# Recommender tower on one core: a quarter's pieces in another order on every engine, norms between bias and variance, the last layers five quarters sooner

## What is computed

```python
e = stack([tbl_f[ids[:, f]] for f in range(26)], axis=1)     # (2048, 26, 64)
x = layer_norm(dense @ Wd.T, gd, bd)                         # (2048, 128)
y = layer_norm(einsum('bnd,ed->bne', e, Ws), gs, bs)         # per sample and feature
y = einsum('bne,pn->bep', y, Wsi)                            # 26 features mixed to 32
y = swapaxes(layer_norm(y, gsi, bsi), 1, 2)
T = concatenate([x[:, None, :], y], axis=1)                  # (2048, 33, 128)
Z = einsum('bnd,bmd->bnm', T, T)                             # pairwise products
z = layer_norm(Z[:, TRIL_I, TRIL_J] @ Wl.T, gl, bl)[:, :384]
h = concatenate([z, dense], axis=1)
h = maximum(h @ W_top1 + b_top1, 0.0)
h = maximum(h @ W_top2 + b_top2, 0.0)
out = h @ W_top3                                             # (2048, 1)
```

## Time and profile before

| | |
|---|---|
| median of 3 runs | 1021.42 us (1021.18 to 1025.5) |
| the profiled execution | 1019.76 us, its span 1018.0 us |
| busy in the span | PE 657.4 us (65%), PEld 474.9 (47%), DVE 530.4 (52%), ACT 279.4 (27%), POOL 423.3 (42%) |
| mean granted TensorE clock | 0.79 |
| DMA | 20.19 MB, mean 20 GB/s |

### The profile page before, as it was taken

The page is one execution under the profiler, slowest core; times in us unless marked ns, Lnnn a source line. Parts: engine busy times, 40 slices in busy tenths (PEclk is TensorE's granted clock), DMA queues, the critical chain, the costliest instruction groups (busy, mean ns, idle before and its releaser), DMA issues.

```text
span 1018.0 us, 17199 instructions
## 1 busy us (share of the span) xinstructions
PE 657.4 (65%) x6955; PEld 474.9 (47%) x6955; DVE 530.4 (52%) x769; ACT 279.4 (27%) x666; POOL 423.3 (42%) x422
## 2 busy tenths in 40 slices
PE   2034535364767757677775767768577776788887
PEld 2033324243444534446453545545355454566566
DVE  2248455454654535465453546545355654588740
ACT  1201122122232322233231323322132332345332
POOL 6757534545443344543345453433545343300000
PEclk9999676686776768777676778767687776799899
DMA  6111001010000011100001110000110010000000
GB/s 163 32 19 27 19 15 20 19 21 17 15 20 14 18 19 21 19 13 18 14 19 19 22 18 13 19 14 19 19 22 16 13 21 14 14 3 2 1 2 1
DMA packets 22606, 20.19 MB, mean 20 GB/s; under 512 B 12016, under 2 KB 14720, under 8 KB 22528
## 3 DMA queue, kind: packets, MB, share of 16 engines
q0 software_dynamic: 13312, 13.66, 7.4%
q1 hardware_dynamic: 8400, 4.33, 1.7%
q10 hardware_dynamic: 816, 1.11, 0.3%
HBM read 19.07 MB, written 0.01 MB: 19 GB/s over the span
## 4 chain that ended last, share of the span: by engine, by line
another core or an unknown queue 29%; PE 27%; issue 22%; DVE 14%; ACT 7%; ACTq 0%; DVEq 0%; POOL 0%; POOLq 0%
PE b_y L340 6%; PE b_l L416 5%; PE b_a L319 4%; DVE yb L781 3%; PE b_l L394 3%; DVE byn L776 2%; PE b_z L352 2%; ACT sq L508 2%; PE b_l L423 2%; DVE nrm L767 2%; PE b_mix L328 2%; DVE prod L747 1%; PE b_a L310 1%; ACT embt L492 1%
## 5 line engine op out<-in xcount | busy, mean ns | idle before, releaser
L253 POOL DMA_INDIRECT emb<-in_tbl,idx x416 | 422.6, 1016 | 453.7 <-DVE nrm L767 333.5
L319 PE MATMUL b_a<-gram_w,embt 128*128 128x128 f32 x416 | 85.3, 361 | 135.6 <-ACT embt L492 65.1
L793 DVE RECIPROCAL rstd_y<-std_y 128x32 f32<-128x32 f32 x64 | 21.2, 331 | 270.0 <-ACT std_y L513 269.9
L352 PE MATMUL b_z<-V 128*32 128x34 f32 x4096 | 91.3, 206 | 96.7 <-issue 89.6
L319 PEld LDWEIGHTS b_a<-gram_w,embt 128*128 128x128 f32 x416 | 71.9, 257 | 149.6 <-ACT embt L492 76.4
L508 ACT ACTIVATE sq<-yb 128x1024 f32<-128x1024 f32 x64 | 67.7, 1057 | 265.8 <-DVE yb L781 219.7
L328 PE MATMUL b_mix<-mix,byn 128*128 128x128 f32 x512 | 103.3, 334 | 39.8 <-issue 38.9
L352 PEld LDWEIGHTS b_z<-V 128*32 128x32 f32 x4096 | 67.6, 114 | 121.7 <-issue 107.8
L788 DVE TENSOR_REDUCE var_y<-sq 128x32 f32<-128x1024 f32 x64 | 78.1, 1220 | 71.9 <-ACT sq L508 47.2
L328 PEld LDWEIGHTS b_mix<-mix,byn 128*128 128x128 f32 x512 | 88.5, 239 | 48.3 <-issue 47.4
L340 PE MATMUL b_y<-mixed,projw 64*128 64x512 f32 x256 | 99.2, 862 | 15.2 <-ACT mixed L503 14.9
(11 more groups left out here) (131 smaller groups left out, 759.2 us busy)
## 6 DMA issues: line engine op xcount, KB each, us to landing
emb<-in_tbl,idx POOLq DMA_INDIRECT x416
dense<-in_r_dense_t SPq DMA_DIRECT2D x16, 128.0 KB
V<-in_L_rec_Wl ACTq DMA_DIRECT2D x1, 1056.0 KB
w<-in_W_top SPq DMA_DIRECT2D x2, 512.0 KB
w<-in_W_top SPq DMA_DIRECT2D x1, 768.0 KB
out_y<-y_sb SPq DMA_DIRECT2D x16, 0.5 KB
idx<-in_ids SPq DMA_DIRECT2D x1, 195.0 KB
wd<-in_L_rec_Wd SPq DMA_DIRECT2D x1, 128.0 KB
```

Source lines behind the costliest of these rows:

```text
L253: pool.indirect_dma_start(out=emb[t % 2][:, f, :], out_offset=None, in_=tables[f], in_offset=bass.IndirectOffsetOnAxis(ap=idx[:, t, f:f + ...
L319: last = nc.tensor.matmul(b_a[:, n * P:(n + 1) * P], embt[:, n, :], gram_w[:, :], start=True, stop=True)
L352: last = nc.tensor.matmul(b_z[32 * q:32 * q + 32, GRAM * j:GRAM * (j + 1)], v[:, 0:NP], v, start=True, stop=True)
```

## The change

No instruction is added or removed; the same ones run in another order and under other waits.

- PE: `mix_features` ahead of `transposes`; `gram` of the previous part is no longer last but stands ahead of `project`; `interact_back` directly behind `project`, ahead of `norms`; `layer3` ahead of `interact`.
- DVE: `add_bias`, then `norms` and `bound_n`, then `variance`, then `normalize` of the half just measured, `by_sample`'s second part, and `scale` of the same part, in the same quarter. `shuffle` is cut in two calls, the second at the start of the next quarter; `by_sample` too.
- ACT: `copy_mixed` ahead of `copy_embt`; `copy_zs`, `scale_x`, `scale_o` and `copy_z` ahead of `square_y`; `deviation_y` of the same part behind it.
- The constants: PAIRS 12 to 11, INTERACT 13 to 12, INTERACT_NORM 14 to 13, with `interact_back` in that quarter, LAYER1 18 to 13, LAYER2 20 to 15, LAYER3 21 to 16, STORE 22 to 17: 78 quarters in place of 83. `dt` has 4 buffers in place of 5, `xt` 2 in place of 3, and the waits that protect shared banks follow.

The core of the diff:

```diff
-PAIRS = 12
-INTERACT = 13
-INTERACT_NORM = 14
-INTERACT_BACK = 15
-LAYER1 = 18
-LAYER2 = 20
-LAYER3 = 21
-STORE = 22
+PAIRS = 11
+INTERACT = 12
+INTERACT_NORM = 13
+LAYER1 = 13
+LAYER2 = 15
+LAYER3 = 16
+STORE = 17
...
             def dense_back(t):
                 pe.wait_ge(xn_done, t + 1)
+                after(pe, zt_copied, 2 * (t - 1))
...
             def pair_rows(t):
 
                 pe.wait_ge(zb_ready, 3 * (t + 1))
-                after(pe, zz_copied, t)
+                after(pe, h1_relued, 4 * (t - 1) + 2)
...
-                if ab:
-                    transposes(*ab)
                 if bc:
                     mix_features(*bc)
                 if ab:
-                    norms(*ab)
+                    transposes(*ab)
+                if cc:
+                    gram(*cc)
                 if bc:
                     project(*bc)
+                if (t := tile(h, INTERACT_NORM)) is not None:
+                    interact_back(t)
+                if ab:
+                    norms(*ab)
...
                 if (t := tile(h, DENSE)) is not None:
                     dense_project(t)
-                if cc:
-                    gram(*cc)
...
+            def by_sample(t, k):
...
+                if (t := tile(h, INTERACT_NORM)) is not None:
+                    scale_o(t)
                 if (t := tile(h, DENSE)) is not None:
                     copy_dt(t)
+                if (t := tile(h, INTERACT_NORM)) is not None:
+                    copy_z(t)
                 if bc:
                     square_y(*bc)
                 if ab and ab[1] % 2:
                     deviation_n(ab[0], ab[1] // 2)
+                if bc:
+                    deviation_y(*bc)
...
                 if (t := tile(h, DENSE_NORM)) is not None:
                     moments_x(t)
-                    normalize(t, 0)
                 if (t := tile(h, SHUFFLE)) is not None:
-                    normalize(t, 1)
-                    shuffle(t)
-                if cc:
-                    scale(*cc)
+                    shuffle(t, 1)
+                if (t := tile(h, PAIRS)) is not None:
+                    by_sample(t, 0)
                 if (t := tile(h, INTERACT_NORM)) is not None:
                     recip_o(t)
                 if (t := tile(h, DENSE_NORM)) is not None:
                     recip_x(t)
+                if bc:
+                    add_bias(*bc)
+
                 if ab:
                     norms(*ab)
                     if ab[1] % 2:
                         bound_n(ab[0], ab[1] // 2)
                 if bc:
-                    add_bias(*bc)
                     variance(*bc)
+
+                if ab and ab[1] % 2:
+                    normalize(ab[0], ab[1] // 2)
+                if (t := tile(h, PAIRS)) is not None:
+                    by_sample(t, 1)
+                if bc:
+                    scale(*bc)
+                if (t := tile(h, SHUFFLE - 1)) is not None:
+                    shuffle(t, 0)
```

More of the change, by code:

```diff
@@ L359, in dense_transposes @@
                 after(pe, x_copied, 2 * t)
-                after(pe, zt_copied, 2 * (t - 2))
                 for f in range(2):
@@ L369, in dense_project @@
                 for f in range(2):
-                    last = nc.tensor.matmul(b_x[:, 2 * P:3 * P], dt[t % 5][:, f, :], wdt[:, f, :], start=(f == 0), stop=(f == 1))
+                    last = nc.tensor.matmul(b_x[:, 2 * P:3 * P], dt[t % 4][:, f, :], wdt[:, f, :], start=(f == 0), stop=(f == 1))
                 last.then_inc(x_projected, 1)
@@ L406, in layer1 @@
                 pe.wait_ge(zz_copied, t + 1)
-                if k == 0:
-                    pe.wait_ge(zt_copied, 2 * min(t + 2, T))
-                    after(pe, y_copied, t)
-                else:
-                    pe.wait_ge(z_ready, min(t + 2, T))
                 for m in (2 * k, 2 * k + 1):
@@ L453, in _ @@
                     pair_rows(t)
+                if (t := tile(h, LAYER3)) is not None:
+                    layer3(t)
                 if (t := tile(h, INTERACT)) is not None:
                     interact(t)
-                if (t := tile(h, LAYER3)) is not None:
-                    layer3(t)
                 if (t := tile(h, LAYER1)) is not None:
                     layer1(t, 0)
-                if (t := tile(h, INTERACT_BACK)) is not None:
-                    interact_back(t)
                 if (t := tile(h, LAYER1 + 1)) is not None:
@@ L498, in deviation_n, with deviation_y, deviation_x, deviation_o @@
                 nc.scalar.activation(std_n[:, f[0]:f[-1] + 1], var_m[:, f[0]:f[-1] + 1], ACT.Sqrt, bias=eps[:, 0:1]).then_inc(stdn_done, 1)
+            def deviation_y(t, c):
+                act.wait_ge(vary_done, 4 * t + c + 1)
+                after(act, rstdy_done, 4 * t + c - 1)
+                nc.scalar.activation(std_y[c % 2][:, :], var_y[c % 2][:, :], ACT.Sqrt, bias=eps[:, 0:1]).then_inc(stdy_done, 1)
+            def deviation_x(t):
+                act.wait_ge(x_step, 2 * (t + 1))
+                after(act, x_rstd, t)
+                nc.scalar.activation(sd_x[:, :], mv_x[:, 1:2], ACT.Sqrt, bias=eps[:, 0:1]).then_inc(x_std, 1)
+            def deviation_o(t):
+                act.wait_ge(o_step, 2 * (t + 1))
+                after(act, o_rstd, t)
+                nc.scalar.activation(sd_o[:, :], mv_o[:, 1:2], ACT.Sqrt, bias=eps[:, 0:1]).then_inc(o_std, 1)
             def copy_mixed(t, c):
@@ L508, in square_y @@
                 nc.scalar.activation(sq[:, :, :, :], yb[c % 2][:, :, :, :], ACT.Square, scale=NP ** -0.5).then_inc(y_squared, 1)
-            def deviation_y(t, c):
-                act.wait_ge(vary_done, 4 * t + c + 1)
-                after(act, rstdy_done, 4 * t + c - 1)
-                nc.scalar.activation(std_y[c % 2][:, :], var_y[c % 2][:, :], ACT.Sqrt, bias=eps[:, 0:1]).then_inc(stdy_done, 1)
             def copy_zs(t, c):
@@ L540, in copy_x @@
                 after(act, gram_done, 4 * (t - 1))
-                after(act, zt_done, 2 * (t - 2))
+                after(act, zt_done, 2 * (t - 1))
                 if t == 1:
@@ L547, in copy_x @@
                                      ).then_inc(x_copied, 1)
-                nc.scalar.activation(xt[t % 3][:, :], src, ACT.Identity, scale=gd[:, 0:1], bias=bd[:, 0:1]).then_inc(x_copied, 1)
+                nc.scalar.activation(xt[t % 2][:, :], src, ACT.Identity, scale=gd[:, 0:1], bias=bd[:, 0:1]).then_inc(x_copied, 1)
             def copy_zt(t):
@@ L555, in copy_zt @@
                 nc.scalar.activation(zt[0:96, 4, :], b_x[0:96, 0:P], ACT.Copy).then_inc(zt_copied, 1)
-            def deviation_o(t):
-                act.wait_ge(o_step, 2 * (t + 1))
-                after(act, o_rstd, t)
-                nc.scalar.activation(sd_o[:, :], mv_o[:, 1:2], ACT.Sqrt, bias=eps[:, 0:1]).then_inc(o_std, 1)
             def scale_o(t):
@@ L617, in _ @@
                     relu1(t, 0)
-                if (t := tile(h, INTERACT_NORM)) is not None:
-                    scale_o(t)
-                if (t := tile(h, INTERACT_BACK)) is not None:
-                    copy_z(t)
                 if (t := tile(h, LAYER1 + 1)) is not None:
                     relu1(t, 1)
-                if (t := tile(h, DENSE_NORM)) is not None:
-                    scale_x(t)
                 if h == 1:
@@ L768, in normalize, with shuffle @@
                                         rstd_n[:, f0:f0 + n].unsqueeze(2).broadcast_to([P, n, D]), ALU.mult).then_inc(nrm_ready, 1)
-            def shuffle(t):
+            def shuffle(t, k):
+                d = slice(k * D // 2, (k + 1) * D // 2)
                 dve.wait_ge(nrm_ready, 2 * (t + 1))
                 after(dve, mix_done, 4 * (t - 1))
-                for k in range(2):
-                    d = slice(k * D // 2, (k + 1) * D // 2)
-                    nc.vector.transpose(byn[t % 2][:, :, d].rearrange("p j d -> p d j"), nrm[:, d, :]).then_inc(byn_ready, 1)
+                nc.vector.transpose(byn[t % 2][:, :, d].rearrange("p j d -> p d j"), nrm[:, d, :]).then_inc(byn_ready, 1)
             def add_bias(t, c):
@@ L838, in _ @@
             for h in range(QUARTERS):
-                ab, bc, cc = part(h, MEASURE), part(h, PROJECT), part(h, PROJECT + 1)
-                if (t := tile(h, PAIRS)) is not None:
-                    by_sample(t)
+                ab, bc = part(h, MEASURE), part(h, PROJECT)
                 if (t := tile(h, INTERACT_NORM)) is not None:
```

57 lines of the change are left out of this document (27 added, 30 removed).

## The result

The changed kernel takes 1085.1 us (median of 4 runs, 1083.7 to 1087.2) where the kernel before takes 1021.3 us (4 runs beside it, 1018.6 to 1025.5): a ratio of 1.062, with a 95% interval of 1.058 to 1.066. The profiled execution has a span of 1084.1 us, against 1018.0.

The account below looks back on a forecast made before the run. No engine's work was the bound; gathers cost some 25 us a tile by making PE's signals behind gram late. Span 1018.0 + 118 (steady tiles) + 7 (after the gathers) - 15 (last layers) = 1128, measured 1131 us, range 1045 to 1185.

Parts of the forecast that it names:

- Steps 1 and 2: Tile without gathers: bare loop 29.0 us plus other pieces in it, 40.2 us in all against 33.9 before.
- step 2: Pieces added to the loop: normalize 4.0, by_sample 1.0, work ahead of gram 2.7, shuffle and layers 3.5 us a tile.
- Step 3: Two gather stretches a tile: project's late signal, behind gram, holds DVE; 29.0 us lost (21 to 34), 25 before.
- Step 4: Steady tile: 69.2 us against 59.3, +9.9 a tile, +118 us over 12.5 tiles less 6.
- Step 5: Eleven quarters after the last gathers: four at +6.3 / 4 each, the others half of that; +7 us (0 to 14).
- Step 6: Last layers sooner: last part's copy to output falls from 44.3 to 29 us, -15 us (-18 to -10).
- Step 7: Queues and buffers: SP's loads and stores, POOL's sooner lots, fewer dt and xt buffers, ACT's order; no further cost.
- Milder: Rival: signals behind gram at their lower bound, loop 38.5, stretches 24, tile 62.5 us; measured 1050 us; chance 0.18.
- Heavier: Rival: project's signal held until each gather stretch ends, tile 75 us; measured 1210 us; chance 0.10.
- cold loop: Rival: PE's matmuls run at half clock without gathers too, tile 77 us; measured 1235 us; chance 0.05.
- Signals come promptly: Rival: project's signal at about 9 us in both stretches, stretches 13, tile 53 us; measured 937 us; chance 0.04.

Follow-up runs that it names:

- experiment 1: Kernel before and changed kernel, both without the gathers of tiles 2 to 15: 670.8 us and 727.4 us.
- experiment 7: Kernel before with the change's loop order alone, layers, normalize and shuffle left in place: 680.8 us, ratio 1.016; without gathers of tiles 2 to 15, 678.3 us.
- experiment 6: Kernel before with only the last layers four quarters sooner: 699.6 us, ratio 1.044; a second placing, with norms between bias and variance: 697.5 us.
- experiment 5: Kernel before with only the norms moved between bias and variance: 670.8 us, ratio 1.001; the same without gathers of tiles 2 to 15: 611.5 us.

## Why the prediction was right in its sign, and where its size came from

The forecast was 1131 us in a range of 1045 to 1185; 1085.1 lies in it, in the lower half: +6.2% where +10.7% was said.

**Steps 1 and 2, the loop:** right in its length. 40.2 us were forecast for a tile without gathers, 40.0 were measured on the first chip (41.3 over another four quarters, from 943.69) and 40.2 on another chip (sum of the medians, experiment 1). How that splits into terms is less sure. The bare loop with everything else left in place is no longer than the kernel before (34.9 us, experiment 7); what makes 40 of it is what step 2 added, the pieces that now stand inside it. The quarter of `interact_back`, where PE waits 3.1 us for z with the norms behind it, was part of a term of 3.5 that also had shuffle and layer 1 in it. The baseline of 33.9 is the shortest four quarters of the trace; by the same parts it is 35.2, and the loop's own loss is 4.8 us a tile and not 6.1. The remark that filling the square's wait gains in DVE's own list and not in this loop holds word for word: alone and without gathers it is worth 59 us, in the changed kernel it is paid back.

**Step 3, the gather stretches:** the mis-sized term, and the step that failed. They cost 63.9 - 40.0 = 23.9 us a tile; 29.0 was forecast, with 21 to 34 around it, and 25.4 is what they cost before. The forecast had them 3.6 us a tile dearer than before, and they are no dearer at all. `project`'s signal came at +12.25 and +12.27 us where 15.5 and 17.0 were taken. That is 8 us less. The early lots of the trace before had said 11.7 and 13.9, and I went above them, because each steady lot before held ACT's signal to the end. That was the wrong row to weigh: there 23 to 27 matmuls lie between the gathers' start and gram, and in the changed kernel gram starts 1.3 us after it. (For the second stretch the sum's own rule, gram at about 2 us and 11.7 or more behind it, gives 13.7 as the lower bound; it said 15.) Of the 8 us only 5.1 show in the tile. Where the other 2.9 went is not taken apart; the norms' signal is late in the second stretch too (4.44 us, not in the sum).

**Step 4, the tile:** +9.9 was forecast, +4.6 came; of the 5.3 between them step 3 accounts for 5.1. Over the run this step was to give +118 and gave 58.8 (1.4 + 55.2 + 2.2). Steps 5 and 6 erred the other way, by 11.0 and 4.4 us, and hid a quarter of that miss.

**Step 5, after the last gathers:** +18.0 against +7 (0 to 14), outside its bounds. The 7 is first of all a slip: four quarters at 6.3 / 4 and seven at half of that are 6.3 + 5.5 = 11.8. Measured between the same copies of `mixed`, the first four quarters take 5.2 us more than before (943.69 to 985.03, before 880.59 to 916.77) and the last seven 8.5 (63.7, before 55.2), 1.2 a quarter and not 0.8. So the extra time fades less than was taken when norms and `normalize` leave. Another 4.4 us lie between the last gather's end and the first of these copies (7.1 us, before 2.8).

**Step 6, the last layers sooner:** -10.6, forecast -15 and within its bounds (-18 to -10); layer 1 to the last output took 10.6 us and not 9, and the layers of the tile before still stood in the way of `pair_rows`. What failed is the sentence beside it: that "while parts still flow they only change which tile's layers are under way" and "cost nothing unless they stand ahead of a gram that is ready". On the other chips the sooner place alone costs 33 us in the steady part for 3.9 in the tail (experiment 6). On the first chip such a cost would be inside the extra 4.8 to 6.1 us of the gather-free tile; it was not taken apart there.

**Step 7:** nothing, and nothing is seen: no wait of PE for features in the changed kernel.

**The signs.** The prediction called itself wrong if yb's waits in the stretches were under 8 us or the gather-free tile under 36 us. The second did not come. The first did, in half of the second stretches: of the 13 waits of each kind from 120.96 on, one of the 14's is under 8 us (6.7 to 11.8) and seven of the 12's (5.1 to 10.2), the 6.68 shown among them. By its own sign, then, the forecast was wrong in the second stretch, which fits step 3. The stretch's DVE work was near to what was said (3.75 and 6.74 us, for 5 and 7).

**Rivals.** *Milder* had the stretches right (24 against 23.9) and the loop wrong (38.5 against 40.0); the time lies between it and the forecast. *Heavier* did not come, and *cold loop* only in a small part: the granted clock is 0.787 over the whole changed kernel, against 0.790 over the kernel before, but without gathers it fell from 1.00 to 0.91 (on another chip 0.99 to 0.93, over 140 and 160 us of experiment 1), where PE is busy 2 us a tile longer, and not the 8 us of that rival. *Signals come promptly* is what four other chips do, and there the change is not faster but slower by 8.8%. The rival forgot that the kernel before gains by prompt signals as well. The Trainium skill ("Runtime: NRT & Kernel Launch", Instruction fetch mechanics) has an engine's instruction supply hidden behind its rate of issue. The later chips agree as far as they can (2 us between the changed kernel with and without gathers, 2.5 in experiment 7). On the first one PE's matmuls come in groups with gaps between them in a gather stretch, but no trace shows whether it is the supply of instructions that is late there.

**What is not settled.** On the first chip the loop's loss is read from the quarters behind the last gathers; its split by parts was measured on other chips, and that it is the same on the first wasn't tried. Why PE's signals are late beside gathers in one session and not in four later ones is open as well; whether it belongs to the chip or to the occasion can't be told from these runs. And the order of experiment 5, worth 59 us where no gather is in the way, wasn't run on the first chip, where gather stretches and loop take turns and it might show.

## What to carry to other kernels

Before moving a step to an earlier quarter, ask for each of its waits how old the awaited result is: in the kernel before, where most results are a quarter old when they are asked for, DVE waits for little but the square, and a wait inside the quarter puts the whole handshake, and all that is queued behind the waiting instruction, into the loop. A wait of 1.1 us on the busiest engine is worth filling, but only as long as what fills it doesn't tie the next step to the same turn. Look at every engine on the way, too: `gram` left the line on PE and stayed in it through a copy on ACT. And when an edit that frees 59 us changes nothing, look for the second limit that stands beside the first; here it was GpSimd's issue of gathers.

## What the runs showed of the hardware

**The same kernel took 1021 us in one session and 670 us in four later ones, on four chips.** The gathers are issued at nearly the same pace in both. The costliest group of the changed kernel on one of the four (busy, mean ns | idle before), to be held against 1015 ns in the result's fence:

```profile
L252 POOL DMA_INDIRECT emb<-in_tbl,idx x416 | 442.6, 1064 | 147.0 <-issue 125.3
```

What differs is that on the first chip PE's signals arrive late in a gather stretch (8.9 and 9.7 us of "remote" ahead of `zs` and `yb`), and that its granted clock is 0.79 against 0.93, where on this one of the four PE is busy 75% of the time and not 59%. I had expected every chip to do as the traced one did, and the forecasts of experiment 1 were too high for that reason.

**A gather of 128 rows costs GpSimd about 1.39 us** (1.09 us and 0.30 us of issue; 1.06 and 0.30 in the changed kernel there, 1.02 and 0.30 on the first chip). 26 of them a tile are a limit of their own, 36.2 us, that no trace of the first chip could show: there GpSimd idled 453.7 us.
